# Centred gate weights, a one-hot matrix that carries each row's deviation, and another order of VectorE's first batch

## What is computed

```python
# x: [4, 512, 512], ctx: [4, 512, 128]
Q, K = ctx @ Wq.T, ctx @ Wk.T
sim = Q @ K.T / (sqrt(32) * 4)                        # per batch [512, 512]
mask = sim >= (the 153rd largest value of its row)    # k = int(0.3 * 512)
A = sigmoid(sim) * mask
A = (A + A.T) / 2
x = x + tanh(g_xattn) * ((1 - gamma) * layernorm(x) + gamma * A)
n = layernorm(x)                                      # (x - mean) / sqrt(var + eps)
probs = softmax(n @ gate_w)                           # 8 experts, the best two are kept
out = sum over the two: share * alpha * (gelu(n @ fc1_w + fc1_b) @ fc2_w + fc2_b)
x = x + tanh(g_ffn) * out
```

## Time and profile before

| | us |
|---|---|
| median of 3 runs | 364.29 |
| span of the profiled execution, first to last instruction | 363.4 |
| PE busy in the span | 324.3 (89%) |
| VectorE busy | 200.7 (55%) |
| ACT busy | 165.0 (45%) |
| GpSimd busy | 100.1 (28%) |

### The profile page before, as it was taken

One profiled execution on the slowest core, in us unless ns is written; L12 is line 12 of the kernel. 1 busy time (PEld: TensorE's weight loads), 2 busy tenths in 40 slices (PEclk: granted clock), 3 DMA queues, 4 the chain that ended last, 5 costly groups with the idle time before them and its releaser, 6 DMA issues.

```text
span 363.4 us, 6131 instructions
## 1 busy us (share of the span) xinstructions
PE 324.3 (89%) x1937; PEld 232.9 (64%) x1937; DVE 200.7 (55%) x697; ACT 165.0 (45%) x384; POOL 100.1 (28%) x141
## 2 busy tenths in 40 slices
PE   6906899779998999899999989999999999999960
PEld 4402667677764786678778576777785877577610
DVE  0488698887879777898886372636206112311010
ACT  2485515389996746256786222232222213132320
POOL 5001001361111357114307431331733111312031
PEclk9975699899999999999999999999999999999996
DMA  2999989977974696876627587744678854533253
GB/s 91 379 392 369 352 298 331 378 267 139 305 145 123 144 243 231 146 161 183 113 54 181 191 173 135 211 100 81 203 163 149 176 119 104 111 64 87 30 74 46
DMA packets 53636, 65.79 MB, mean 181 GB/s; under 512 B 9792, under 2 KB 28512, under 8 KB 53600
## 3 DMA queue, kind: packets, MB, share of 16 engines
q1 hardware_dynamic: 46144, 47.99, 43.7%
q0 software_dynamic: 7456, 17.37, 24.7%
HBM read 39.56 MB, written 25.78 MB: 180 GB/s over the span
## 4 chain that ended last, share of the span: by engine, by line
PE 50%; issue 18%; DVE 14%; DVEq 5%; DMA 5%; POOL 3%; POOLq 2%; ACT 2%; ACTq 0%
PE ps L1711 21%; PE ps L1684 13%; PE ps L1694 10%; DMA out_rows<-ab,dst 3%; PE ps L1647 2%; POOL xs_rows L566 2%; DMA meta<-xs_rows 2%; DVE top L1087 1%; DVE stats L1012 1%; PE ps L1607 1%; PE ps L1721 1%; PE ps L1627 1%; PE ps L1639 1%; POOLq L530 1%; DVEq L1086 1%
## 5 line engine op out<-in xcount | busy, mean ns | idle before, releaser
L1684 PEld LDWEIGHTS ps<-xgT_r,weights 128*128 128x128 f32 x768 | 87.8, 192 | 8.3 <-issue 6.7
L1684 PE MATMUL ps<-xgT_r,weights 128*128 128x128 f32 x768 | 89.6, 276 | 3.6 <-ACT xgT_r L743 2.0
L1711 PE MATMUL ps<-weights,act_r 128*128 128x512 f32 x192 | 86.3, 595 | 1.5 <-ACT act_r L766 1.5
L580 POOL DMA_INDIRECT out_rows<-ys,dst x24 | 37.9, 1578 | 115.2 <-ACT ys L773 70.0
L1711 PEld LDWEIGHTS ps<-weights,act_r 128*128 128x128 f32 x192 | 34.9, 190 | 38.4 <-issue 36.5
L766 ACT ACTIVATE act_r<-ps,b1T 128x128 f32<-128x128 f32 x96 | 27.1, 365 | 38.9 <-PE ps L1684 38.8
L1694 PEld LDWEIGHTS ps<-sim,weights 128*128 128x128 f32 x256 | 35.2, 190 | 1.9 <-issue 1.7
L566 POOL DMA_INDIRECT xs_rows<-ab,pos x32 | 31.9, 998 | 14.5 <-issue 9.1
L1694 PE MATMUL ps<-sim,weights 128*128 128x160 f32 x256 | 35.6, 299 | 0.0
L773 ACT ACTIVATE ys<-ys,meta 128x512 f32<-128x512 f32 x24 | 17.3, 719 | 31.3 <-DVE ys L1322 31.3
L1322 DVE TENSOR_TENSOR ys<-ps,b_r 128x512 f32<-128x512 f32 x24 | 16.5, 686 | 23.4 <-PE ps L1711 22.0
(11 more groups left out here) (206 smaller groups left out, 419.0 us busy)
## 6 DMA issues: line engine op xcount, KB each, us to landing
weights<-in_L_ffn_fc_w SPq DMA_DIRECT2D x16, 1024.0 KB, 8.0
b_r<-in_L_ffn_fc_b SPq DMA_DIRECT2D x32, 256.0 KB, 4.1
xg_r<-xs_rows SPq DMA_DIRECT2D x88, 64.0 KB
xb<-in_x SPq DMA_DIRECT2D x4, 1024.0 KB, 7.1
out_rows<-xb SPq DMA_DIRECT2D x4, 1024.0 KB, 5.5
sim<-xs_rows SPq DMA_DIRECT2D x32, 80.0 KB
xs_rows<-weights SPq DMA_DIRECT2D x1, 2064.0 KB, 13.5
xs_rows<-weights SPq DMA_DIRECT2D x2, 516.0 KB, 5.9
```

What stands on the lines that cost most here:

```text
L580: pool.indirect_dma_start(out=out_rows, out_offset=bass.IndirectOffsetOnAxis(ap=dst[:, k % 2, e:e + 1], axis=0), in_=result_rows(m), in_of ...
L1684: mm = pe.matmul(ps[:, n % 2, i * P:(i + 1) * P], weights[:, e, 0, h, i * P:(i + 1) * P], rows[:, h * P:(h + 1) * P], start=(h == 0), stop ...
L1711: mm = pe.matmul(ps[:, 2 + m % 2, :], rows, weights[:, e, 1, i, :], start=(i == 0), stop=(i == IB - 1))
```

## The change

- The gate weights are centred once, on VectorE: `centre_gate` (four instructions) writes `gate_c`, each weight less its column's mean, in place of `keep_gate_sum` (one instruction). `gate` multiplies by `gate_c` and waits for it once (`gate_ok`).
- `best_two` has no correction any more, in all four batches: the four instructions of L1178 go, and `max` and `max_index` read the logits from PSUM instead of SBUF.
- `x1_var_of(0)` also writes `neg_mean`, and `norm_plain` on ACT subtracts only the mean; it waits for `mean_ok` instead of `bias_ok`. The one-hot matrix carries the row's 1/deviation (`xn_scale`) instead of 1, by a second operation in the same instruction.
- VectorE's order of the first batch. `x_stats(0, 1..3)` go ahead to stand between `sim_stats` and in the first round; `x_var(0)` and `x_scales(0)` move into the second and third. `x_stats(1, 1)` no longer stands between `threshold(0)` and `prove(0)`, and `x_stats(1, 2)`, `x_stats(1, 3)` no longer behind `x1_var_of(0)`; with `x_var(1)` and `sim_stats(1, 0..1)` they now stand behind `next_places(0)`. `best_two(0)` comes directly behind `x1_var_of(0)`, `one_hot(0)` behind `norm(0, 0)`.
- TensorE: `prove(0)` stands ahead of `scores(1, 2)`, and the wait for `m_sb` moves into `project(0)`.

```diff
--- before.py
+++ after.py
@@ -150,8 +150,8 @@
         ones_col = sb("ones_col", [P, 1])
         m_qk = sb("m_qk", [P, C])
         gate_w = sb("gate_w", [P, KB, E])
-        gate_sum = sb("gate_sum", [P, E])
-        logits = sb("logits", [P, BT, E])
+        gate_c = sb("gate_c", [P, KB, E])
+        neg_mean = sb("neg_mean", [P, BT])
         b1T = sb("b1T", [P, E * IB])
         raw = sb("raw", [P, 3])
         alpha_bc = sb("alpha_bc", [P, E])
@@ -258,7 +258,7 @@
         rows_in, b2_in_s = [sem("rows_in0"), sem("rows_in1")], [sem("b2_in0"), sem("b2_in1")]
         meta_in, dst_ok = sem("meta_in"), sem("dst_ok")
         hot_ok, picked_ps, picked_ok = sem("hot_ok"), sem("picked_ps"), sem("picked_ok")
-        bias_ok, plain_ok = sem("bias_ok"), sem("plain_ok")
+        mean_ok, gate_ok, plain_ok = sem("mean_ok"), sem("gate_ok"), sem("plain_ok")
         xgT_ok, hid_ps, act_ok, y_ps, y_sb, ys_ok, added = (
             sem(n) for n in ("xgT_ok", "hid_ps", "act_ok", "y_ps", "y_sb", "ys_ok", "added"))
         over_ok = sem("over_ok")
@@ -731,11 +731,10 @@
 
             def norm_plain(t):
                 if t == 0:
-                    act.wait_ge(bias_ok, 1)
+                    act.wait_ge(mean_ok, 1)
                     act.wait_ge(blank, 16)
                     act.wait_ge(sum_ps, 1)
-                act.activation(plain(t), xb[:, 0, t, :], ACT.Identity, scale=xn_scale[:, t:t + 1],
-                               bias=xn_bias[:, t:t + 1]).then_inc(plain_ok, 1)
+                act.activation(plain(t), xb[:, 0, t, :], ACT.Identity, bias=neg_mean[:, t:t + 1]).then_inc(plain_ok, 1)
 
             def picked(e):
                 act.wait_ge(picked_ps, e + 1)
@@ -1159,11 +1158,13 @@
                 for t in range(BT):
                     dve.bn_aggr(mv1[:, t, :], stat1[:, t, :])
                 dve.drain().then_inc(x1_var, 1)
+                if b == 0:
+                    dve.tensor_scalar(neg_mean[:], mv1[:, :, 0], -1.0, None, ALU.mult).then_inc(mean_ok, 1)
 
             def norm_bias(b):
                 dve.wait_ge(x1_rstd, b + 1)
                 dve.scalar_tensor_tensor(xn_bias[:], xn_scale[:], -1.0, mv1[:, :, 0], ALU.mult, ALU.mult)
-                dve.drain().then_inc(bias_ok, 1)
+                dve.drain()
 
             def norm(b, t):
 
@@ -1175,14 +1176,10 @@
                 dve.drain()
                 dve.wait_ge(gate_ps, BT * (b + 1))
                 for t in range(BT):
-                    dve.scalar_tensor_tensor(logits[:, t, :], gate_sum[:], mv1[:, t, 0:1], logit_ps[:, t, :], ALU.mult,
-                                             ALU.add)
+                    dve.max(out=best[:, t, :], in_=logit_ps[:, t, :])
                 dve.drain()
                 for t in range(BT):
-                    dve.max(out=best[:, t, :], in_=logits[:, t, :])
-                dve.drain()
-                for t in range(BT):
-                    dve.max_index(out=best_i[:, t, :], in_max=best[:, t, :], in_values=logits[:, t, :])
+                    dve.max_index(out=best_i[:, t, :], in_max=best[:, t, :], in_values=logit_ps[:, t, :])
                 dve.drain()
                 dve.tensor_copy(idx_f[:], best_i[:, :, 0:PICKS])
                 dve.drain()
@@ -1239,8 +1236,8 @@
                                              ALU.add, ALU.mult)
                     dve.drain()
                 for t in range(BT):
-                    last = dve.tensor_scalar(xg_r[:, e, t * P:(t + 1) * P], place_no[:], chosen[:, t, e:e + 1], None,
-                                             ALU.is_equal)
+                    last = dve.tensor_scalar(xg_r[:, e, t * P:(t + 1) * P], place_no[:], chosen[:, t, e:e + 1],
+                                             xn_scale[:, t:t + 1], ALU.is_equal, ALU.mult)
                 last.then_inc(hot_ok, 1)
 
             def next_places(b):
@@ -1325,32 +1322,35 @@
 
                 return x1T[:, 0, :]
 
-            def keep_gate_sum():
+            def centre_gate():
                 dve.wait_ge(sum_ps, 1)
-                dve.tensor_scalar(gate_sum[:], total_ps, -1.0, None, ALU.mult)
+                for k in range(KB):
+                    last = dve.scalar_tensor_tensor(gate_c[:, k, :], total_ps, -1.0 / D, gate_w[:, k, :], ALU.mult, ALU.add)
+                last.then_inc(gate_ok, 1)
 
             coefficients()
             x_stats(0, 0)
-            for t in range(BT):
-                sim_stats(0, t)
+            sim_stats(0, 0)
+            x_stats(0, 1)
+            sim_stats(0, 1)
+            x_stats(0, 2)
+            sim_stats(0, 2)
+            sim_stats(0, 3)
             first_guess(0)
-            keep_gate_sum()
+            centre_gate()
             count(0, 0)
-            x_stats(0, 1)
+            x_stats(0, 3)
             narrow(0, 0)
             count(0, 1)
-            x_stats(0, 2)
+            x_var(0)
             narrow(0, 1)
             count(0, 2)
-            x_stats(0, 3)
-            x_var(0)
+            x_scales(0)
             narrow(0, 2)
-            x_scales(0)
             x_stats(1, 0)
             for t in range(BT):
                 largest(0, t)
             threshold(0)
-            x_stats(1, 1)
             prove(0)
             for t in range(BT):
                 mask(0, t)
@@ -1361,23 +1361,24 @@
             for t in range(BT):
                 x1_stats(0, t)
             x1_var_of(0)
-            x_stats(1, 2)
-            x_stats(1, 3)
+            best_two(0)
             norm_bias(0)
             norm(0, 0)
+            one_hot(0)
+            gaps(0)
             norm(0, 1)
-            best_two(0)
             norm(0, 2)
             norm(0, 3)
-            x_var(1)
-            sim_stats(1, 0)
-            gaps(0)
-            sim_stats(1, 1)
-            one_hot(0)
             shares(0)
             one_hot(1)
             places(0)
             next_places(0)
+            x_stats(1, 1)
+            x_stats(1, 2)
+            x_stats(1, 3)
+            x_var(1)
+            sim_stats(1, 0)
+            sim_stats(1, 1)
             x_scales(1)
             sim_stats(1, 2)
             sim_stats(1, 3)
@@ -1595,6 +1596,8 @@
 
             def project(b):
                 pe.wait_ge(ctxT_sb, b + 1)
+                if b == 0:
+                    pe.wait_ge(m_sb, 1)
                 pe.matmul(ps[:, CTX_BANK, :], m_qk[:], ctxT[:], start=True, stop=True).then_inc(q_ps, 1)
 
             def scores(b, t):
@@ -1643,8 +1646,10 @@
             def gate(b, t):
                 i = b * BT + t
                 pe.wait_ge(x1T_sb, i + 1)
+                if i == 0:
+                    pe.wait_ge(gate_ok, 1)
                 for k in range(KB):
-                    mm = pe.matmul(logit_ps[:, t, :], x1T[:, t % 2, k * P:(k + 1) * P], gate_w[:, k, :], start=(k == 0),
+                    mm = pe.matmul(logit_ps[:, t, :], x1T[:, t % 2, k * P:(k + 1) * P], gate_c[:, k, :], start=(k == 0),
                                    stop=(k == KB - 1))
                 mm.then_inc(gate_ps, 1)
 
@@ -1753,7 +1758,6 @@
             pe.wait_ge(qk_in, 32)
             pe.matmul(ps[:, 0, 0:C], wq, wk, start=True, stop=True).then_inc(m_ps, 1)
             turn_context(0)
-            pe.wait_ge(m_sb, 1)
             project(0)
             for t in range(BT):
                 scores(0, t)
@@ -1765,8 +1769,8 @@
             scores(1, 0)
             scores(1, 1)
             busy_to_threshold()
+            prove(0)
             scores(1, 2)
-            prove(0)
             scores(1, 3)
             keep_busy(BUSY_MASK)
             project(2)
```

## The result

The changed kernel takes **370.12 us** (median of 4, 367.3 to 372.53) against 364.91 us (median of 4, 364.28 to 367.03) in the same session: ratio 1.0131, 95% interval 1.0087 to 1.0175. In a second session, 10 runs against 33 of the kernel before, it was 1.0140 (1.0093 to 1.0187). The forecast was 366.5, within 363.8 to 368.5, "within 1%". It had the right sign, the right first place (VectorE's late `x_scales(1)`) and less than half of the size: 2.2 us instead of 5.2.

The account below looks back on a forecast made before the run. VectorE's late x_scales(1), through ACT's list, sets the first expert; TensorE's work follows. VectorE +0.9 and clock +2.1, less 0.8 swallowed, gave 363.4 + 2.2 = 365.6; plus 0.9, 366.5 us, range 363.8 to 368.5.

Parts of the forecast that it names:

- the proof's gain: VectorE's read of the proof's number: about 41.35 instead of 43.21, -1.85, with prove(0) ahead of scores(1, 2).
- the first expert's clock loss of 2.1: TensorE at layer1(0, 0): slow clock after more than nine microseconds idle costs +1.6 to +2.6, taken as +2.1.
- the signs named in advance for a wrong main step: Main step wrong if x_scales(1) ends before 71.4 or L1684 begins before 78.5.
- V: Stretch from the second layernorm's variance to the end of x_scales(1); the forecast placed these at 55.1 and 72.3.
- wait for `rank` +0.1: VectorE's list between variance and x_scales(1): waiting for TensorE's rank adds only 0.1 us.
- `add` and the second variance come 1.2 us earlier: VectorE behind the proof: second variance ready at 55.1 instead of 56.3, as TensorE reaches the third transposes earlier.
- The +0.4 for `max` and `max_index`: VectorE's best_two: reading PSUM costs 0.06 more for each of eight instructions, +0.4 us, bounds 0 and +0.5.
- rival B: Longer slow stretch or late scattered rows make TensorE wait before the third expert: another 1.8, 368.3; chance 0.17.
- the median of the runs is 0.9 above the span: Last step of the sum: 0.9 us added to the forecast span of 365.6 to give the median.
- A (the clock no loss): TensorE's clock stays at 2.4 GHz or returns at once, so VectorE's +0.9 decides: 365.2; chance 0.17.
- C (the waits swallow the delay): Waits at 147.25 and 213.55 swallow up to 2.44 of TensorE's delay: 364.2, not slower; chance 0.16.
- D: Picked rows decide: first expert at 71, then TensorE waits for scattered rows, no faster than 364; no chance of its own.

Follow-up runs that it names:

- a2_order: Kernel before with the changed kernel's orders and the old arithmetic; 370.25 us, ratio 1.0156.
- b4_early_only: Changed kernel with its new order only up to threshold(0) and the early prove(0), VectorE's later list as before; 363.35 us, ratio 0.9956.
- c1_picked_first: Changed kernel with picked(0) and picked(1) moved ahead of affine_x(1) in ScalarE's list; 369.41 us, ratio 1.0131.
- b3_after_again: The changed kernel without an edit, run once more; 369.57 us, ratio 1.0140.
- a3: Changed kernel with x_stats(1, 1) back before prove(0), and x_stats(1, 2), x_stats(1, 3), x_var(1) before best_two(0); 368.37 us, ratio 1.0105.
- a4: Changed kernel with 124 matmuls that compute nothing between pick_rows(1) and layer1(0, 0); 368.80 us, ratio 1.0122.
- c3: Changed kernel with 8 filler matmuls behind each of gate(1, 0..2), batch 1 alone; 369.16 us, ratio 1.0102.
- b1_after_dense: Changed kernel with 8 filler matmuls behind each of gate(0, 0..2) and gate(1, 0..2); 367.25 us, ratio 1.0062.
- c2: Changed kernel with keep_busy(12) and rank(0) ahead of scores(2, 0) and scores(2, 1) on TensorE; 367.36 us, ratio 1.0071.
- a1: Changed kernel's arithmetic alone, with the orders of the kernel before; 362.76 us, ratio 0.9958.
- c4: b4_early_only with picked(0), picked(1) ahead of affine_x(1) and gelu(0, 0) ahead of signs(1, 1) on ScalarE; 366.67 us, ratio 1.0052.

## Why the prediction was right or wrong

**Right: where and why, at the first step.** VectorE's late `x_scales(1)` sets ScalarE's `affine_x(1)`, `signs(1, 0)`, `picked` and the first expert (a2_order against b4_early_only, and c1_picked_first for ScalarE's list). The wait of 2.2 for the gates was 2.05, the proof's gain is there (from the last score statistic to the number 23.4 us instead of 25.5), GpSimd's late scatters are hidden (`layer1` of the third expert has no wait of its own), the first expert's clock loss of 2.1 was 1.77 here and 1.99 in b3_after_again. The part swallowed up to the second half of `adjacency` was 1.05 (3.49 late at the first `layer2`, 2.44 there), forecast 0.8. All the signs named in advance for a wrong main step stayed away; they did not look at the places that failed.

**Luck: +2.44 at `adjacency` against +2.2.** This execution was 1.9 us ahead at VectorE's last score statistic (its end at 15.84 instead of 17.74), before anything that the forecast prices. The first eight scores took 3.86, against 6.28 in the profile of before, which had half the clock there. Counted from that mark `x_scales(1)` ends 3.6 later than before, not 0.9: the early part brought nothing where -1.2 was forecast, and V was 1.55 longer than forecast. The start hid 1.9 of these 2.7.

**Wrong: "wait for `rank` +0.1".** It was 1.67, and 1.59 to 2.39 in the profiles of a2, a3, a4, b3, c1 and c3. I had taken TensorE's scores at full speed there. The kernel before had no such delay (1.96 for its four scores), and its `x_stats(1, 2..3)`, `norm`s and other work ahead of `chosen` would have hidden one, as b4_early_only shows; taking them away laid open two waits one behind the other, not one. **"`add` and the second variance come 1.2 us earlier"** was nothing in this profile: from the last score statistic to the variance 38.5 us in both kernels. VectorE waited 1.04 and 1.30 for the transposes, and TensorE was late with them while the scores behind the early proof ran at the lower clock (3.78 us for four at 39.15). In the other profiles with the new early order this length is 36.7 to 38.6, with the old one 37.9 and 38.4. **The one-hot's second operation,** for which the sum has no time, took +0.24 for each expert. **The +0.4 for `max` and `max_index`, which "now read PSUM",** was +0.03: from `max` to the next step 1.20 us against 1.17. The wait, the one-hots and the reads miss by +1.57, +0.48 and -0.37, 1.68 together; V was forecast as 17.2 (55.1 to 72.3) and measured 18.75.

Both prices for reading PSUM came from one row, L1178 (0.62 for four). But `centre_gate` (L1328) reads PSUM over 8 columns with the same kind of instruction, and four take 0.37, so the forecast's +0.46 there was about +0.23 (0.51 us from its start to the next step, against 0.28). L1178 has a scalar for each row, L1328 has not, and the one-hots became longer with such a scalar too, each by about 0.06 us. That this scalar, and not PSUM, was the price in L1178 is a reading of these rows; no run isolates it.

The Trainium skill ("VectorE: DVE Perf Modes", the section on the TRN2 errata) gives an instruction 120 fixed cycles with a PSUM source and 58 with one in SBUF, at 0.96 GHz; an estimate from that page would be +0.5 us for the eight instructions. The rows with 8 columns do not show it (0.39 against 0.37 for the four `max`), and the measurement decides.

**Wrong, and the largest part: there is no step for the clock beyond the first expert.** I followed the granted clock where TensorE idles. It also fell between 124.9 and 131.8, where TensorE's rows show no gap over 0.24 us: 2.8 us net of TensorE's path here. None of the cases had it; rival B has nearly the time (368.3), but by another mechanism, a wait for the third expert's rows, that did not come.

The Trainium skill ("TensorE: Matmul & The Clock Gate", Part 1: The HAM clock gate) says that the gate follows how busy the engine has been. The trace of this stretch calls it busy all along and shows the clock at half; b1_after_dense, where filler stands behind the gates, shows it whole. So a row that shows TensorE busy does not say that the clock stays up. The Trainium skill, in the same section, puts the ramp under 1% of a typical span, from which the forecast's estimate was 3.6 us at most; it is passed here: 1.8 at the first expert and 2.8 at the gates.

**Wrong: "the median of the runs is 0.9 above the span".** The profiled execution of the changed kernel took 368.69 with a span of 367.0, 1.7 apart, and in all the runs the two are 1.7 to 1.9 apart. My base was 0.8 too low. The miss of 3.6 adds up: 0.8 for this, 1.4 for the span (367.0 against 365.6), and 1.4 because the profiled execution lay that far under its own median. Without the lucky start of 1.9 the span's own miss is about 3.3, and the change costs 5.5 from that mark to the end, near the 5.2 between the medians.

**Rivals.** A (the clock no loss) is out by the 9.15 us of the first expert, C (the waits swallow the delay) since TensorE is 5.2 late at 152 and the wait at 217 took only 0.9 of that, D since the first expert came at 80.28 and not at 71.

**Small slips.** The bounds named for the forecast's own range give 365.3 to 367.5, not 365.5 to 367.6, and a mean of 0.58 puts the fall of the clock in the kernel before at 22.2, not 22.4.

**Open.** Why the clock falls at the gates of one kernel and not of another. In batch 0 it goes with the new early order, in all ten profiles without filler there. Why the fall at batch 1's gates goes with the late order. It is in the profiles of the change, a3, a4, b3 and c2; not in those of a1, b4, c4 and before, with the old late order; but not in a2 and c1 either, which have the new one. So it isn't a property of the order alone: the instructions there are the same in all, only their moments differ, by some microseconds. One profile for each kernel doesn't give its frequency. Nor is this fall the whole of the excess: the profiled execution of c1_picked_first had none and took 369.31, with its slow stretch on `layer2` and longer waits in batch 0 (2.52 and 2.39, V 20.0) in its place.
